# Last attention: weights mixed through differences, one whole subtraction, and the mixing at the end of VectorE's step

## What is computed

```python
pooled = hidden_states.mean(axis=1)
logits = jax.nn.relu(pooled @ Wg1 + bg1) @ Wg2 + bg2
vals, idx = jax.lax.top_k(logits, TOP_K)            # TOP_K = 2 of NUM_EXPERTS = 4
sm = jax.nn.softmax(vals, axis=-1)
weights = jnp.zeros_like(logits).at[jnp.arange(B)[:, None], idx].set(sm)
def moe_proj(W, b):
    Wc = jnp.einsum('be,ecd->bcd', weights, W)
    bc = weights @ b
    return jnp.einsum('btc,bcd->btd', hidden_states, Wc) + bc[:, None, :]
...
scores = jnp.einsum('bthd,bshd->bhts', q, k) / np.sqrt(D).astype(np.float32)
attn = jax.nn.softmax(scores, axis=-1)
out = jnp.einsum('bhts,bshd->bthd', attn, v).reshape(B, T, C)
return out @ Wo + bo
```

## Time and profile before

| | us |
|---|---|
| runs shown, median | 2094.26 |
| lowest and highest of 3 | 2084.05, 2097.2 |
| the profiled execution | 2082.72 |
| its span, first to last instruction | 2081.0 |

### The profile page before, as it was taken

How to read it: one execution, slowest core, us unless ns; L and a number is a source line. 1 busy time by engine, 2 the same in 40 slices (tenths; PEclk the granted TensorE clock), 3 DMA queues, 4 the chain that set the end, 5 groups by cost and what they waited for, 6 DMA issues and landing times. The chain is left out here.

```text
span 2081.0 us, 79977 instructions
## 1 busy us (share of the span) xinstructions
PE 1834.5 (88%) x31023; PEld 1447.4 (70%) x31023; DVE 1624.5 (78%) x3910; ACT 1311.1 (63%) x3796; POOL 1158.5 (56%) x1556
## 2 busy tenths in 40 slices
PE   5999977989999969999989996899887573799998
PEld 4777754657888858888867763777776452677776
DVE  6988877867888868888856667677565787799998
ACT  4677775655666656666545544555554583699997
POOL 6777744875555435555568873753564275233332
PEclk9999987999999989999999996999999786899999
DMA  5222212002222157000011110134562530000000
GB/s 129 54 54 53 55 34 61 1 20 71 69 76 65 39 85 29 1 1 1 1 28 41 39 30 21 44 134 142 199 202 95 154 99 17 2 19 19 19 19 24
DMA packets 185355, 116.73 MB, mean 56 GB/s; under 512 B 82556, under 2 KB 177432, under 8 KB 181272
## 3 DMA queue, kind: packets, MB, share of 16 engines
q1 hardware_dynamic: 173656, 74.27, 15.4%
q0 software_dynamic: 8064, 35.97, 4.9%
q10 hardware_dynamic: 3264, 1.38, 0.3%
HBM read 83.28 MB, written 28.27 MB: 54 GB/s over the span
## 5 line engine op out<-in xcount | busy, mean ns | idle before, releaser
L1621 POOL TENSOR_TENSOR L1f_hl<-L1f_h,L1f_hh 128x512 fp32r<-128x512 f32 x128 | 167.3, 1307 | 125.6 <-DVE L1f_hh L1633 125.6
L1580 ACT ACTIVATE L1f_h<-L1f_H,L1f_w_b 128x512 f32<-128x512 f32 x192 | 132.4, 690 | 100.9 <-PE L1f_H L1033 95.4
L412 POOL TENSOR_TENSOR L3f_wide<-L3f_flat,head_of_row 128x512 f32<-128x512 f32 x64 | 67.2, 1051 | 187.5 <-PE L3f_S L487 168.7
L1633 DVE CAST L1f_hh<-L1f_h 128x512 fp32r<-128x512 f32 x192 | 125.9, 662 | 33.5 <-ACT L1f_h L1580 31.6
L2006 DVE TENSOR_TENSOR L2f_both_h<-L2f_both_G,L2f_both_act 128x512 f32<-128x512 f32 x114 | 78.7, 690 | 90.9 <-ACT L2f_both_act L1981 70.4
L1981 ACT ACTIVATE L2f_both_act<-L2f_both_A 128x512 f32<-128x512 f32 x114 | 68.2, 598 | 119.6 <-PE L2f_both_G L1033 85.9
L1898 POOL DMA_INDIRECT token_y<-L1f_w_w,L2f_both_token x88 | 90.2, 1025 | 73.7 <-DVE L1f_w_w L2025 50.9
L412 POOL TENSOR_TENSOR L1a_wide<-L1a_flat,head_of_row 128x512 f32<-128x512 f32 x64 | 66.7, 1042 | 110.8 <-ACT L1a_flat L695 110.8
L719 DVE TENSOR_REDUCE L1a_mx<-L1a_S 128x16 f32<-128x1024 f32 x64 | 78.4, 1225 | 55.3 <-PE L1a_S L487 55.3
L971 DVE COPY_PREDICATED L2a_weights<-L2a_mask_raw,L2a_S 128x1024 f32<-128x1024 int32 x64 | 86.5, 1352 | 14.6 <-PE L2a_S L888 14.6
L621 ACT ACTIVATE L1a_probs_T<-L1a_PT 128x512 f32<-128x512 f32 x64 | 38.2, 597 | 94.3 <-PE L1a_PT L451 94.3
(11 more groups left out here) (560 smaller groups left out, 6842.2 us busy)
## 6 DMA issues: line engine op xcount, KB each, us to landing
L0a_mask_raw<-mask SPq DMA_DIRECT2D x256, 32.0 KB, 2.0
expert_split<-L1a_split_halves SPq DMA_DIRECT2D x7, 1152.0 KB, 6.1
L2f_both_xhat<-sorted_x SPq DMA_DIRECT2D x22, 258.0 KB
sorted_x<-L1f_zero SPq DMA_DIRECT2D x4, 1408.0 KB, 22.9
L0a_ctxT<-ctx_T SPq DMA_DIRECT2D x64, 64.0 KB, 1.9
L1a_ctxT<-ctx_T SPq DMA_DIRECT2D x64, 64.0 KB, 1.9
L1a_mask_raw<-mask SPq DMA_DIRECT2D x256, 0.1 KB
L2a_ctxT<-ctx_T SPq DMA_DIRECT2D x64, 64.0 KB, 2.2
```

Of the source, the lines that this page charges most:

```text
L412: pool.tensor_tensor(wide[:, s], flat[:, s, :].rearrange("p (b n) -> p b n", b=B2).unsqueeze(2).broadcast_to([P, B2, 4, S]), c.head_of_row ...
L1580: act.activation(h[:, q % 3, :], psH[:, q % 2, :], ACT.Relu, bias=b1[:, q:q + 1]).then_inc(h_kept, 1)
L1621: pool.tensor_tensor(hl[:, q % 3, :], h[:, q % 3, :], hh[:, q % 3, :], ALU.subtract).then_inc(hl_pool, 1)
L1633: dve.tensor_copy(hh[:, q % 3, :], h[:, q % 3, :]).then_inc(hh_made, 1)
```

## The change

The mixed weights are now the second expert's plus the first gate times the difference of the two experts' weights, as the gates add up to one. GpSimd makes the six differences between experts (`moe["less"]`, shown as w_less) once, during the gate stage. The gate stage writes, in place of the first expert's offset, that of the pair's difference, and one weight per batch in place of two; its VectorE work changes by a few small instructions. ScalarE's scaled copies and its loads of offsets go; VectorE loads two pairs of offsets per tile. ScalarE takes over the copy of `xT` and makes the normalized x ahead of the second exponential. VectorE subtracts in one instruction and does the mixing last in its step, behind reciprocal, division and sum into x.

```diff
@@ attention, allocation
         if moe:
-            Wa, Wc = sb("weights_first", [P, RING, B2, 3 * P]), sb("weights_both", [P, RING, B2, 3 * P])
-            wa_made, wc_made, stored = sem("wa_made"), sem("wc_made"), sem("stored")
+            Wc = sb("weights_both", [P, RING, B2, 3 * P])
+            wc_made, stored = sem("wc_made"), sem("stored")
             w_all = w["all"][:, :, :, :].rearrange("p e j n -> p (e j n)")
+            w_less = moe["less"][:, :, :].rearrange("p q n -> p (q n)")
@@ ScalarE's step
-                if moe:
-                    for u, s in at(i, r, 0):
-                        _, first_at = nc.values_load_multi_w_load_instructions(
-                            moe["at"][0:1, 0, bass.ds(B2 * u, B2)], engines=(mybir.EngineType.Activation,),
...
-                if moe:
-                    for u, s in at(i, r, 0):
-                        wait(act, wc_made, u - 3)
-                        act.activation(Wa[:, s, 0, :], w_all[:, bass.ds(first_at[0], 3 * P)], ACT.Copy,
-                                       scale=moe["two"][:, 0, bass.ds(B2 * u, 1)])
...
-                if not moe:
-                    for u, s in at(i, r, 1):
...
+                for u, s in at(i, r, 1):
+                    wait(act, xT_done, u + 1)
+                    wait(act, v_done if moe else qk_done, u - 3)
+                    act.activation(xT[:, s, :], psTY[:, 0:P], ACT.Copy).then_inc(xT_kept, 1)
...
-                if moe:
-                    for u, s in at(i, r, 0):
-                        act.activation(Wa[:, s, 1, :], w_all[:, bass.ds(first_at[1], 3 * P)], ACT.Copy,
-                                       scale=moe["two"][:, 0, bass.ds(B2 * u + 1, 1)]).then_inc(wa_made, 1)
+                for u, s in at(i, r, 0) if moe else ():
+                    wait(act, xT_done, u - 3)
+                    act.activation(xhat[:, s, :], c.x[:, u, :], ACT.Identity, bias=c.nmr[:, bass.ds(u, 1)],
+                                   scale=c.rstd[:, bass.ds(u, 1)]).then_inc(xhat_made, 1)
                 for u, s in at(i, r, 5):
                     wait(act, pt1_done, u + 1)
                     act.activation(PT[:, s % 2, 4:8, :].rearrange("p g n -> p (g n)"), psPT[:, :], ACT.Exp
                                    ).then_inc(pt1_kept, 1)
-                for u, s in at(i, r, 0) if moe else ():
...
@@ VectorE's step
                     for u, s in at(i, r, 1):
-                        _, second_at = nc.values_load_multi_w_load_instructions(
+                        _, pair_at = nc.values_load_multi_w_load_instructions(
+                            moe["at"][0:1, 0, bass.ds(B2 * u, B2)], engines=(mybir.EngineType.DVE,),
...
+                        _, last_at = nc.values_load_multi_w_load_instructions(
...
-                        wait(dve, xT_done, u + 1)
-                        wait(dve, v_done, u - 3)
-                        dve.tensor_copy(xT[:, s, :], psTY[:, 0:P]).then_inc(xT_kept, 1)
...
+                    if moe:
+                        dve.tensor_tensor(less[:, s % 2].rearrange("p (g j) k -> p g j k", j=4), S4,
+                                          mx4.unsqueeze(3).broadcast_to([P, 4, 4, S]), ALU.subtract
+                                          ).then_inc(less_made, 2)
+                        continue
...
-                if moe:
-                    for u, s in at(i, r, 1):
-                        wait(dve, wa_made, u + 1)
-                        for b in range(B2):
-                            last = dve.scalar_tensor_tensor(
-                                out=Wc[:, s, b, :], in0=w_all[:, bass.ds(second_at[b], 3 * P)],
-                                scalar=moe["two"][:, 1, bass.ds(B2 * u + b, 1)], in1=Wa[:, s, b, :],
-                                op0=ALU.mult, op1=ALU.add)
-                        last.then_inc(wc_made, 1)
...
                     dve.tensor_tensor(c.x[:, u, :], psY, c.x[:, u, :], ALU.add).then_inc(x_summed, 1)
+                if moe:
+                    for u, s in at(i, r, 1):
+                        wait(dve, v_done, u - 3)
+                        for b in range(B2):
+                            last = dve.scalar_tensor_tensor(
+                                out=Wc[:, s, b, :], in0=w_less[:, bass.ds(pair_at[b], 3 * P)],
+                                scalar=moe["two"][:, bass.ds(B2 * u + b, 1)],
+                                in1=w_all[:, bass.ds(last_at[b], 3 * P)], op0=ALU.mult, op1=ALU.add)
+                        last.then_inc(wc_made, 1)
@@ mixture_gates
+        @block.gpsimd
+        def _(pool):
+            for l in range(1, E):
+                for f in range(l):
+                    pool.tensor_tensor(moe["less"][:, l * (l - 1) // 2 + f, :],
+                                       w_all[:, f, :, :].rearrange("p j n -> p (j n)"),
+                                       w_all[:, l, :, :].rearrange("p j n -> p (j n)"), ALU.subtract
+                                       ).then_inc(less_made, 1)
+            pool.wait_ge(less_made, E * (E - 1) // 2)
```

57 lines of the change are left out of this document (28 added, 29 removed).

## The result

The changed kernel takes 2109.48 us (median of 10 runs) against 2089.71 us before (10 runs): the ratio on record is 1.0107, 95% interval 1.0089 to 1.0124, or some 22 us slower (0.0107 x 2089.71). It is not the quotient of the two medians, which are 19.8 us apart (1.0095). The forecast was 2110 us; the range 2092 to 2121 us holds the time. The prediction called one per cent the limit of what can be told from no change.

What follows compares the result with a forecast made beforehand. A loop through four engines, with mixing and widening taking turns, was to bound the last attention: 58 steps at 4.72 instead of 4.40 us, +18.6, start -2.0, gate 0, together +16.6 us on the median 2094.26: 2110 us, range 2092 to 2121.

Steps and rivals of the forecast that it cites:

- The loop: Last attention: a chain through VectorE, TensorE, ScalarE and GpSimd holds each step at 4.72 us, before 4.40; chance 0.75.
- the rival to the first link: Ahead of q and k: TensorE waits for ScalarE's copy of transposed x, not the mixed weights; raised after measuring, no chance given.
- q and k: Loop term: TensorE's eight products for q and k take 1.00 us.
- The turns: VectorE's mixing and GpSimd's widening and addition exclude each other: 1.15 us from the widening's end to the mixing's end.
- The order: In each step of the last attention GpSimd's widening starts first, 0.49 us ahead of VectorE's mixing.
- The second load of offsets: VectorE's added load before each subtraction lies under the maxima; taken as nothing, at most 1.14 us.
- The start: Start of the last attention: the first mixing comes earlier, -2.0 us of 0 to -3.1.
- The gate: Gate stage: VectorE's two first products may meet GpSimd's differences, 0 to +2.1 us, against small operations saved; taken as 0.
- No clash: Rival for the last attention: the engines' own work decides, step 4.14 us, time 2077 us; chance 0.10.
- Full durations: Rival: a blocked instruction begins only when the other has ended, step 5.25 us, time 2141 us; chance 0.03.
- The addition keeps the turn: Rival: GpSimd's addition goes directly behind the widening, before the mixing; step 4.94 us, time 2123 us; chance 0.07.
- The gain and the clash cancel: Rival: the step stays near 4.40 us and only the start is gained, 2092 us; chance 0.05.

Runs made afterwards that it cites:

- e7: Changed kernel without GpSimd's addition of the output bias to x and VectorE's wait for it: step 4.63 us, 2076.29 us in a single run.
- e4: Changed kernel, GpSimd's widening no longer waits for the normalized x, its addition waits instead: step 4.46 us, ratio 1.0007 to the kernel before.
- e6: Changed kernel, ScalarE copies the transposed x ahead of the transposed output instead of behind it: step 4.83 us, 2099.58 us in a single run.
- e5: Changed kernel, first mixing instruction moved between maxima and subtraction, second left at the end: step 4.27 us, ratio 0.9951 to the kernel before.
- e8: Changed kernel, mixing split around the subtraction, normalized x ahead of the four copies, gate differences behind VectorE's first products: step 4.26 us, ratio 0.9934 to before.
- e12: Changed kernel, mixing split around the subtraction, widening not waiting for normalized x, gate differences behind VectorE's first products: step 4.29 us, ratio 0.9931 to before.
- e11: Changed kernel with the subtraction of the maxima in two halves again: step 4.83 us, 2113.05 us in a single run.
- e1: Changed kernel, GpSimd's widening and addition replaced by fills that read nothing: step 4.25 us, 2038.75 us, ratio 0.9940 to the kernel before.
- e2: Changed kernel, ScalarE makes the normalized x behind the second exponential again, last in its step: step 4.34 us, ratio 0.9967 to the kernel before.
- e3: Changed kernel, VectorE mixes ahead of reciprocal, division and sum into x again: step 4.93 us, ratio 1.0114 to the kernel before.
- e9: Changed kernel, mixing ahead of the reciprocal and normalized x behind the second exponential again: step 4.49 us, ratio 1.0005 to the kernel before.
- e10: Kernel before the change, with the normalized x made directly behind the copies of q and k: step 4.42 us, ratio 1.0015 to the kernel before.

## Why the prediction was right, step by step

- **The loop.** The forecast's chain of eight terms is the one in the trace. Two of its links were moved one at a time: e7 took out the addition's turn (0.20 us less, 0.21 expected), e4 the normalized x (0.37 less, 0.40 expected, with VectorE's own work then setting the pace). e6 moved the rival to the first link and changed nothing.

| term | predicted | measured |
|---|---|---|
| mixing end to TensorE | 0.14 | 0.14 |
| q and k | 1.00 | 1.08 |
| to ScalarE | 0.04 | 0.04 |
| four copies | 0.79 | 0.80 |
| normalized x | 0.48 | 0.51 |
| to GpSimd | 0.08 | 0.07 |
| widening | 1.04 | 1.04 |
| turns | 1.15 | 1.15 |
| sum | 4.72 | 4.83 |

- **The terms that were mis-sized** are q and k, 0.08 us, and the normalized x, 0.03 us. The 1.00 us of the earlier trace rows was of a TensorE that came from other work and had its weight load behind it. In the changed kernel, where it has stood waiting for the weights, it takes 1.08; in steps of e5, e8 and e12 without that wait it is 1.00 again. That the wait itself lengthens it is my reading and wasn't tried apart. The loop goes round some 60 times, so 0.11 us were 6.6 us, and with them the forecast's +16.6 us become +23. That is what the traces have (+23.6).
- **The time itself** came within 0.5 us of the forecast, and that is luck. The forecast was +16 us on 2094.26, the median of the three runs shown; ten runs of the kernel before have 2089.71. A start 4.6 us too high and a loss some 4 to 7 us too small cancel. What was right is the loop and its size to 2%.
- **The turns**, the term on which all hung, came from a single start-up meeting in the earlier trace rows and held to 0.01 us in the steady step. So did the addition's 0.77 us and the second mixing's 0.81. The first mixing takes 1.04 us instead of the expected 0.99, as it starts 0.42 and not 0.49 us after the widening.
- **The order.** The widening was to start 0.49 us ahead of the mixing; it is 0.42 us (1939.19, 1939.61). The widening comes 0.11 us later, by the two terms above. VectorE comes 0.04 us later too, which gives so much back: maxima to subtraction takes 1.31, not 1.27 us (1936.47 to 1937.78). The second load of offsets isn't the reason: in e11, with the same two loads and the subtraction in halves, it is 1.24 us:

```profile
1917.93 1.21 DVE L705 TENSOR_REDUCE L3f_mx<-L3f_S 128x16 f32<-128x1024 f32 x1
1919.17 0.69 DVE L722 TENSOR_TENSOR L3f_less_max<-L3f_S,L3f_mx 128x512 f32<-128x512 f32 x1
```

- **The second load of offsets**, which I had priced at nothing, takes 0.53 us and did cost nothing in the changed kernel. It isn't free in a faster step, as e5 shows: there the loads lengthen every fourth step by about 0.4 us.
- **The start** gained 1.9 us (2.0 expected). **The gate** moved by 0.03 us (0 expected), but as two amounts that cancelled: the two products took 1.13 and 1.08 us beside GpSimd's differences, 1.6 us more than before together, within the bound of +2.1. With GpSimd's differences held back (e8) the gate is 1.07 us shorter, so that much of it reached the time. What gave it back isn't the small operations from the logits to the offsets (4.36 us before, 4.40 in the changed kernel). The part from the offsets to the fill became 0.67 us shorter, with a copy of 128 instead of 256 columns in it; where the rest comes from is open.
- **The rivals.** "No clash" (2077 us) is what e1 makes of it, in which the reads of GpSimd are left out (0.9940 x 2089.71 = 2077). "Full durations" (5.25 us) fell: see the last section. "The addition keeps the turn" (4.94) fell too, with 1.15 us and the mixing ahead of the addition in each steady step. "The gain and the clash cancel" (a step near 4.40) fell with 4.83: no mixing slipped in ahead of the widening there.
- **What the prediction had incomplete** is the share of the two moves. It spoke of both as bringing the instructions together. e2, e3 and e9 show that the early normalized x does the harm in either place of the mixing, and e10 that it does none in the old step; the change would have gained about 0.3% without that one move (e2).

## What to carry to other kernels

Before an instruction with two SBUF operands is moved on VectorE, look at what GpSimd does at the new place, and at who starts first: in these runs a meeting was paid by the one that came second, and mattered only if that one was in the loop. A load of offsets into registers is work too: it cost nothing under a slack loop and a tenth of a microsecond per step in a tight one. An instruction whose data are there (here the widening, which waited for a normalized x that it doesn't read) shouldn't be tied to another engine's later work. Where two candidates for a wait end within 0.01 us, move the one the profile names before believing it.
